# An attention and convolution kernel on one Trainium2 core: prob x val in two bursts of four key chunks instead of four bursts of two

## What is computed

```python
def _L0_conv_ref(x, Wq, bq, Wk, bk, Wv, bv):          # on _gn(x), group norm
    t = x.reshape(B, C, S).transpose(0, 2, 1)         # B=8, C=512, S=1024
    q = t @ Wq.T + bq; k = t @ Wk.T + bk; v = t @ Wv.T + bv
    q = q.reshape(B * NUM_HEADS, S, hd)               # a plain reshape: 8 groups an image, hd=64
    ...
    scores = jnp.einsum('gqd,gkd->gqk', q, k) / jnp.sqrt(hd)
    attn = jax.nn.softmax(scores, axis=-1)
    wv = jnp.einsum('gqk,gkd->gqd', attn, v)
x = x + _L0_conv_ref(_gn(x), ...)
x = x + _L1_conv_ref(_gn(x), ...)                     # masked 3x3 convolution
```

## Time and profile before

| | |
|---|---|
| time, 3 runs | 2692.41, 2693.74 (median), 2695.08 us |
| profiled execution | 2691.37 us, its span 2689.6 us |
| mean granted TensorE clock | 0.984 of 2.4 GHz |
| busy: PE, DVE, POOL, ACT | 95%, 77%, 44%, 40% of the span |
| first stage, second stage | to about 1931 us, to the end |

### The profile page before, as it was taken

How to read it: one execution, slowest core, us unless ns; L and a number is a source line. 1 busy time by engine, 2 the same in 40 slices (tenths; PEclk the granted TensorE clock), 3 DMA queues, 4 the chain that set the end, 5 groups by cost and what they waited for, 6 DMA issues and landing times.

```text
span 2689.6 us, 38766 instructions
## 1 busy us (share of the span) xinstructions
PE 2546.9 (95%) x11312; PEld 998.1 (37%) x11312; DVE 2069.7 (77%) x2832; ACT 1088.5 (40%) x1801; POOL 1170.0 (44%) x907
## 2 busy tenths in 40 slices
PE   5999999999999999999999999976699999999998
PEld 2333333333333333333333333321244444444443
DVE  5887787787788788778878868789868968968614
ACT  3455455455544545544554554443323132122100
POOL 3356466556555655654655564665603003003000
PEclk9999999999999999999999999998799999999999
DMA  5224243241423414324143330531164553744534
GB/s 147 82 74 114 65 125 84 58 133 58 113 83 91 113 45 126 96 65 122 55 118 87 94 107 19 140 100 52 60 230 172 219 203 126 268 155 140 189 107 159
DMA packets 209768, 309.00 MB, mean 115 GB/s; under 512 B 80272, under 2 KB 129552, under 8 KB 209552
## 3 DMA queue, kind: packets, MB, share of 16 engines
q1 hardware_dynamic: 209552, 306.36, 36.8%
HBM read 202.88 MB, written 52.69 MB: 95 GB/s over the span
## 4 chain that ended last, share of the span: by engine, by line
PE 81%; DVE 11%; issue 4%; POOL 2%; ACT 1%; DMA 1%; DVEq 0%; SPq 0%; ACTq 0%; POOLq 0%
PE bank L760 28%; PE bank L667 14%; PE bank L655 13%; PE bank L612 11%; PE bank L630 7%; PE bank L622 5%; DVE nmax L1156 4%; DVE prob_sum L1150 2%; PE bank L644 2%; POOL prob_sum L997 1%; DVE nt L211 1%; DVE rstd L214 1%; DVE nt L209 1%; PE bank L638 1%; ACT prob L842 1%
## 5 line engine op out<-in xcount | busy, mean ns | idle before, releaser
L1156 DVE TENSOR_REDUCE nmax<-bank 128x1 f32<-128x512 f32 x1024 | 660.8, 684 | 213.9 <-PE bank L630 205.2
L842 ACT ACTIVATE prob<-bank 128x512 f32<-128x512 f32 x1024 | 555.9, 596 | 656.2 <-PE bank L655 649.9
L997 POOL TENSOR_TENSOR prob_sum<-prob_sum,prob 128x512 f32<-128x512 f32 x384 | 565.0, 1471 | 448.4 <-ACT prob L842 446.5
L760 PE MATMUL bank<-v,u_slab 128*128 128x512 f16 x3456 | 749.2, 380 | 3.4 <-DVE v L1324 3.4
L667 PE MATMUL bank<-prob,val 128*64 128x512 f32 x2048 | 501.9, 608 | 2.3 <-ACT prob L842 2.3
L760 PEld LDWEIGHTS bank<-v,u_slab 128*128 128x128 f16 x3456 | 338.7, 98 | 412.9 <-DVE v L1324 5.1
L630 PE MATMUL bank<-k_a,q_a 128*128 128x512 f16 x1024 | 389.9, 386 | 39.2 <-DVE nmax L1156 34.4
L1150 DVE TENSOR_TENSOR prob_sum<-prob_sum,prob 128x512 f32<-128x512 f32 x384 | 386.9, 1008 | 13.1 <-DVE shift L1166 8.7
L655 PE MATMUL bank<-q_a,k_a 128*128 128x512 f16 x1024 | 318.1, 385 | 19.0 <-ACT prob L842 16.9
L655 PE MATMUL bank<-q_b,k_b 128*128 128x512 f16 x1024 | 308.8, 384 | 5.4 <-DMA q_b<-shift 5.3
L1048 POOL TENSOR_TENSOR t_a<-tab_mem 128x1224 f32<-128x1224 f32 x16 | 50.1, 3130 | 446.7 <-DVEq L1273 434.4
(11 more groups left out here) (119 smaller groups left out, 2633.6 us busy)
## 6 DMA issues: line engine op xcount, KB each, us to landing
u_slab<-u_scratch SPq DMA_DIRECT2D x72, 1024.0 KB, 5.0
tile<-x_scratch SPq DMA_DIRECT2D x34, 1024.0 KB, 7.8
xs<-x SPq DMA_DIRECT2D x28, 1024.0 KB, 5.7
u_scratch<-u_w SPq DMA_DIRECT2D x96, 192.0 KB, 2.8
q_a<-qk_hi SPq DMA_DIRECT2D x64, 256.0 KB, 4.8
den_sb<-recip_scratch SPq DMA_DIRECT2D x128, 128.0 KB, 2.9
x_scratch<-xr SPq DMA_DIRECT2D x16, 1024.0 KB, 4.4
xr<-x SPq DMA_DIRECT2D x15, 1024.0 KB, 8.1
```

What stands on the lines that cost most here:

```text
L760: mm = pe.matmul(bank_at(pos, co)[:].rearrange("p (i n) -> p i n", i=2), slab[:, l, c, co * P:(co + 1) * P], image[v][:, 2 * c:2 * c + 2, ...
L842: act.activation(prob[:, (2 * u + e) % 8], sc_bank[bank_turn(s * 16 + 2 * u + e, 16 * HPI)[0]][:], ACT.Exp, scale=float(D) ** -0.5).then_i ...
L997: nc.gpsimd.tensor_tensor(acc, in0, prob[:, (2 * kc + 1) % 8], ALU.add).then_inc(s1["sum1"], 1)
L1156: dve.tensor_reduce(nmax[:, m // 2, m % 2:m % 2 + 1], src[:], AX.X, ALU.max, negate=True)\
```

## The change

- `weigh_pair` becomes `weigh_half`: chunks 0 to 3 in one burst at the end of `u=4`, chunks 4 to 7 in one at the end of `u=0` of the next slot. The bursts in `u=2` and `u=6` are gone.
- A fifth place `"e"` behind the burst of `u=0` holds the denominator, on PE and on DVE; it was in `u=2`.
- `prob` has five pairs. `PROB_AT` gives the pair of each chunk: 0, 1, 2, 3, 4, 1, 2, 3. `LAST_IN` says whose matmul and sum a pair must have seen before ACT writes it again.
- `psum_acc` has one set; POOL's first addition of a slot waits until the denominator has been copied (`den_out`).
- ACT copies the result bank (`evacuate_pv`) behind the exponentials of `u=1`, before of `u=0`.
- The first image's normalised input goes to `xr[1]`.

```diff
+PROB_AT = [0, 1, 2, 3, 4, 1, 2, 3]
+LAST_IN = [(1, 0), (1, 5), (1, 6), (1, 7), (1, 4), (0, 1), (0, 2), (0, 3)]
...
-    if prev and u == 2:
-        at["d"].append(("den", 0))
+    at["e"] = [("den", 0)] if prev and u == 0 else []
...
-        prob = sb(st1, "prob", [P, 8, 512], F32)
-        psum_acc = sb(st1, "prob_sum", [P, 2, 2, 512], F32)
+        prob = sb(st1, "prob", [P, 10, 512], F32)
+        psum_acc = sb(st1, "prob_sum", [P, 2, 512], F32)
...
-            def weigh_pair(h, s, n):
-
-                weigh(h, s, 2 * n)
-                weigh(h, s, 2 * n + 1)
+            def weigh_half(h, s, n):
+
+                for kc in range(4 * n, 4 * n + 4):
+                    weigh(h, s, kc)
...
                     if u == 0 and prev:
-                        weigh_pair(h - 1, (s - 1) % HPI, SEG // 2 - 1)
-                    if u >= 2 and u % 2 == 0:
-                        weigh_pair(h, s, u // 2 - 1)
-
-            pe.sem_inc(s1["pv_done"], 8)
+                        weigh_half(h - 1, (s - 1) % HPI, 1)
+                    if u == 4:
+                        weigh_half(h, s, 0)
+                    run("e")
+
+            pe.sem_inc(s1["pv_done"], 16)
...
-                act.wait_ge(s1["pv_done"], 16 * h + 2 * u + e + 1)
-                act.wait_ge(s1[f"sum{e}"], 7 * h + (u + 4 if u < 4 else 7 + max(u - 4, 1)))
-                act.activation(prob[:, (2 * u + e) % 8], ...
+                ago, kc = LAST_IN[u]
+                act.wait_ge(s1["pv_done"], 16 * h + 16 * (1 - ago) + 2 * kc + e + 1)
+                act.wait_ge(s1[f"sum{e}"], 7 * h + 7 * (1 - ago) + max(kc, 1))
+                act.activation(prob[:, 2 * PROB_AT[u] + e], ...
...
-                    if u == 0 and prev:
+                    if u == 1 and prev:
                         evacuate_pv(h - 1)
...
+                if kc == 1 and prev:
+                    pool.wait_ge(s1["den_out"], h)
...
-                    for place in "abcd":
+                    for place in "abcde":
```

More of the change, by code:

```diff
@@ L265, in build @@
         q_av, q_bv = ([v[half][:].rearrange("p (j e) t -> p e j t", e=2) for half in range(2)] for v in (q_a, q_b))
-        stage = prob[:].rearrange("p (a k) n -> p a k n", a=2)
+        stage = prob[:, 0:8].rearrange("p (a k) n -> p a k n", a=2)
         PER_RING = HPI * (16 + 1 + 1) + 2 * HPH + 2
@@ L638, in shift_item, with den_item @@
                 pe.matmul(dst[0:SEG, 0:TOK], nmin[:], ident, start=True, stop=True).then_inc(s1["ring_full"], 1)
-            def den_item(h, par):
+            def den_item(h):
                 dst = take()
                 pe.wait_ge(s1["sum0"], 7 + 7 * (h + 1))
-                pe.matmul(dst[0:D, :], ones, psum_acc[:, par, 0], start=True, stop=True)
+                pe.matmul(dst[0:D, :], ones, psum_acc[:, 0], start=True, stop=True)
                 pe.wait_ge(s1["sum1"], 7 + 7 * (h + 1))
-                pe.matmul(dst[D:P, :], ones, psum_acc[:, par, 1], start=True, stop=True).then_inc(s1["ring_full"], 1)
+                pe.matmul(dst[D:P, :], ones, psum_acc[:, 1], start=True, stop=True).then_inc(s1["ring_full"], 1)
             def scores(h, s, u, part):
@@ L667, in weigh @@
                     pe.matmul(pv_bank[e * D:(e + 1) * D, :], val[s // HPH][:, s % HPH, kc * D:(kc + 1) * D],
-                              prob[:, (2 * kc + e) % 8], start=(kc == 0),
+                              prob[:, 2 * PROB_AT[kc] + e], start=(kc == 0),
                               stop=(kc == SEG - 1)).then_inc(s1["pv_done"], 1)
-            def weigh_pair(h, s, n):
-                weigh(h, s, 2 * n)
-                weigh(h, s, 2 * n + 1)
+            def weigh_half(h, s, n):
+                for kc in range(4 * n, 4 * n + 4):
+                    weigh(h, s, kc)
             def slot(img, s, prev=True, nxt=True, more=True):
@@ L811, in normed @@
                 if first:
-                    dst = psum_acc[:, c // 2, c % 2]
+                    dst = xr[1][:, c]
                     if half == 1:
@@ L991, in _, with add_tile @@
         def _(pool):
-            def add_tile(h, s, kc):
+            def add_tile(h, s, kc, prev=True):
                 pool.wait_ge(s1["exp_done"], 4 + 16 * h + 2 * kc + 2)
-                acc = psum_acc[:, s % 2, 1]
+                acc = psum_acc[:, 1]
                 pool.wait_ge(s1["sum1"], 7 + 7 * h + kc - 1)
+                if kc == 1 and prev:
+                    pool.wait_ge(s1["den_out"], h)
                 in0 = prob[:, 1] if kc == 1 else acc
-                nc.gpsimd.tensor_tensor(acc, in0, prob[:, (2 * kc + 1) % 8], ALU.add).then_inc(s1["sum1"], 1)
+                nc.gpsimd.tensor_tensor(acc, in0, prob[:, 2 * PROB_AT[kc] + 1], ALU.add).then_inc(s1["sum1"], 1)
             def divide(h):
@@ L1067, in slot @@
                     if u >= 2:
[L1068 removed]
+                        add_tile(h, s, u - 1, prev)
                     if u == 6 and prev:
@@ L1130, in split_norm @@
             def split_norm(img, half, c, first=False):
-                src = psum_acc[:, c // 2, c % 2] if first else xn32[:]
+                src = xr[1][:, c] if first else xn32[:]
                 k = 4 * half + c
@@ L1146, in add_tile @@
                 dve.wait_ge(s1["exp_done"], 4 + 16 * h + 2 * kc + 1)
-                acc = psum_acc[:, s % 2, 0]
+                acc = psum_acc[:, 0]
                 dve.wait_ge(s1["sum0"], 7 + 7 * h + kc - 1)
                 in0 = prob[:, 0] if kc == 1 else acc
-                dve.tensor_tensor(acc, in0, prob[:, (2 * kc) % 8], ALU.add).then_inc(s1["sum0"], 1)
+                dve.tensor_tensor(acc, in0, prob[:, 2 * PROB_AT[kc]], ALU.add).then_inc(s1["sum0"], 1)
             def max_item(h, m):
```

10 lines of the change are left out of this document (5 added, 5 removed).

## The result

The changed kernel takes 2806.3 us (median of four runs, 2805.24 to 2811.14), the kernel before, measured beside it, 2694.4: a ratio of 1.0422, 95% interval 1.041 to 1.0434, 112 us slower. The prediction said slower (0.86), with 61 us; 2806 lies above its range, which ended at 2788.

What follows compares the result with a forecast made beforehand. PE's own work was taken to set the time, with DVE just behind it in slots without projection. Terms 34 - 4 + 9 + 13 + 9 = +61 us on 2691.37 gave 2752 us, range 2693 to 2788.

Steps and rivals of the forecast that it cites:

- rival 3: Clock falls behind waits in slots without projection, so the next burst's 3.4 us double: 48 us more, 2798; chance 0.08.
- `s=6` ... +1.3, +9 us: Value-projection slot `s=6`: PE reaches the ring 2.8 us earlier and waits for DVE; +1.3 a slot, +9 us.
- The same value projection in `s=2` adds 2. Net +1.8, +13 us: `s=0` to `s=2`: denominator wait and value projection, less the old 1.36 us wait and its neighbour; +13 us, seven images.
- Loss 2.4 us. Fourteen such slots: +34 us: Slots without projection (`s=3`, `s=7`): 19.1 us PE work plus 4.0 waits, against 20.7 before; +34 us.
- the shift: Slots without projection: shift row's chain takes 6.1 us, PE arrives in 4.3; new wait 1.8 us.
- `s=4`, `s=5`: -0.3 each: Slots `s=4`, `s=5`: PE has 10 us more and DVE catches up; -4 us together over seven images.
- The last image ... +9 us: Last image: DVE is the bound from `s=3`, each denominator adds a round trip of 1.2 us; +9 us, 0 to 16.
- 64 x 0.26 = 16.5 us: Two of four bursts go, saving one way in and out per group: 16.5 us, or 33 if leaving the shift tile is free.
- the fifth `prob` pair and the single `psum_acc` cost nothing: Buffers: PE order alone already frees them in time, and needed sums are the same distance back; cost nothing.
- POOL's new wait ... is met: POOL's wait for `den_out` is met, as its first addition stands two units later.
- only the shift's wait is real: Rival: fourteen slots lose 1.5 us, the rest gains 13 us; 2700, 2686 to 2715; chance 0.12.
- PE stays the bound: Rival: other engines' waits stay hidden, only burst transitions count; -16.5 to -33 us, 2658 to 2675; chance 0.10.

Runs made afterwards that it cites:

- la: Changed kernel with each max-tile reduction reading 128 of its 512 columns: 2700.8 us (1.0036).
- lb: Kernel before with each max-tile reduction reading 128 of its 512 columns: 2654.6 us (0.985).
- f1: f0 with the burst of `u=2` merged into the one of `u=4`: 2811.0 us (1.0443), +75 on f0.
- e4: Changed kernel with DVE writing the shift row ahead of the addition of `u=6`: 2806.2 us (1.0417).
- h3: Kernel before with denominator and copy ahead of the first addition of `u=2`, and POOL's first addition waiting for that copy: 2728.8 us (1.0136).
- f0: Changed kernel with the four old bursts back and the denominator in `u=2` ahead of the additions; five pairs, one sum set: 2736.0 us (1.016).
- h2: Changed kernel with max tiles per unit 3, 2, 3, 2, 3, 3, 0, 0 and the shift row ahead of the addition of `u=6`: 2754.1 us (1.0227).
- g0: Kernel before with the denominator and its copy ahead of the first addition of `u=2`: 2693.0 us (0.9997).

## Why the prediction was wrong

The direction and the place were right: PE's work is all but unchanged, its waits grow in `s=2`, `s=3`, `s=6` and `s=7`, the clock does not fall (0.985 against 0.984, so rival 3 has no part in it), and la against lb shows that what hangs on DVE's reductions is the larger half. Wrong were sizes, 51 us in all, by the prediction's own terms (rounded to whole microseconds):

- **"`s=6` ... +1.3, +9 us" and "The same value projection in `s=2` adds 2. Net +1.8, +13 us".** This is the step that failed most. Measured in the image shown +3.0 in `s=6` and +4.5 in `s=0` to `s=2`, so, for seven such images, 21 and 32 us instead of 9 and 13: **31 of the missing 51**. I counted 2.3 us of waits behind one ring item, the projection of `u=3`. There are five waits and 3.8 us, in `u=1`, `u=3` and `u=4`, with DVE waiting for PE in between. And in `s=2` I set the old wait of 1.36 us against the new ones, but a new one of the same kind came (1.29), and PE waits 2.05 us for DVE's sum ahead of the denominator in `s=2`, longer than what I let the exchange cost. f1 shows that taking out the burst of `u=2` is enough to cause such waits: +75, with 73 in the waits for reductions.
- **"Loss 2.4 us. Fourteen such slots: +34 us".** Measured 3.4 and 2.9, 44 us: 10 missing. PE's own work was right to the digit (19.1), and the sum of waits was near (4.0 predicted, 4.5 found) by luck, since its parts were not: ring 2.4 instead of 1.5, shift 0.8 instead of 1.8, POOL 0 instead of 0.7, and 1.4 us of waits for ACT's exponentials that no term had. The baseline was the other error: 20.7 holds for `s=7`, `s=3` took 20.2. POOL's chain was right (its sum complete at t + 22.2, predicted 21.9); PE came at t + 22.6 instead of 21.2, so it did not wait. The largest part, the shift, cost nothing that could be won back: e4 removed its wait, PE came earlier, and there was the wait for POOL's sum.
- **"`s=4`, `s=5`: -0.3 each".** +0.1 together instead of -0.6: 5 missing. The saving is there, a new wait for ACT takes it.
- **"The last image ... +9 us"**: 21 in the profiles, 12 missing, against which the other images lose 6 us less than seven times the one shown. The longest wait for DVE's sum went from 7.5 to 9.2 us there. I did not take this image apart.
- **"64 x 0.26 = 16.5 us"**: 24 to 26 us, by the 0.37 and 0.4 us a group above. The bounds held. In the sum it stands as 0.3 us a slot, so the difference is small, and it goes against the miss: the change saves PE more than was forecast.
- **"the fifth `prob` pair and the single `psum_acc` cost nothing"** and "POOL's new wait ... is met": the wait is met in the change, by its early denominator. With the denominator in `u=2` that wait, which one sum set requires, costs 35 us (h3). The two parts of the change need each other. The fifth pair was not tried alone; it is somewhere in the 7 to 10 us between h3 and f0.
- Rival 3's time is a slip: 2752 + 48 is 2800, not 2798. Nothing rests on it.

Of the signs named, the windows of 23 us (23.6), the burst of 3.6 (3.59), DVE's idle time ahead of the copy (2.0 in `s=3`, 1.2 to 3.6 over the seven images) and the tile's 0.32 came; PE's share fell by 4 points instead of 2; `s=4` took 30.0, not 29.5.

The rival "only the shift's wait is real" fell with the traces and e4, "PE stays the bound" with the traces. The range was too narrow at its upper end, since it took the one slot that was walked as the worst and let the others differ little. The slots with value projections lost more, and were estimated from a single row.

## What to carry to other kernels

A burst that needs nothing from the other engines is also the time in which they catch up. In a pipeline with a ring as short as three, look at the longest stretch of ring items between two such bursts, not at busy shares: here DVE waited for PE and PE for DVE in one slot in which DVE was busy 68%. When you merge bursts, re-spread the ring's items with them (61 of 112 us here), and walk the slot with the most ring items first. And a wait seen in the trace is a cost only if nothing else ends just behind it: taking away the shift's wait uncovered POOL's sum in e4 and h2. Look for the next release in line, and in the weight loads and the distances of starts too, since overlapping records hide a pause; then test it before you build on it.

## What was unexpected in the hardware

- DVE's addition of two SBUF operands takes 0.68 us by itself and 1.63 when POOL's starts 0.2 us ahead of it; POOL's keeps its 1.27. Over 64 first additions the mean is 1645 ns in h3 and 824 in g0. So here DVE, the engine on the path, is the one that waits. The Trainium skill (SBUF — State Buffer, SBUF: two separate sides) says that the two share a port pair by an exclusive lock, held for the whole instruction; h3's rows agree, with DVE ending 0.55 us after POOL's.
- A busy share can grow by waiting. e4's trace has PE busy 2572.3 us with the same instructions, against 2558.7. The records of the denominator's two halves overlap, so where the second half starts late the engine still counts as busy: together these records cover 85.3 us instead of 74.8, which is most of the difference. The granted clock was 0.980 to 0.982 in e4's four runs and 0.982 to 0.985 in those of the change; what that is worth is not shown.
